# One gather in 64 of the first layer's ring becomes 128 single-row fetches issued by SyncE

## The reference, cut to what matters

```python
def _L0_gnn_ref(features, edge_src, edge_dst, edge_weight, W, b):
    msgs = features[edge_src] * edge_weight[:, None]
    agg = jax.ops.segment_sum(msgs, edge_dst, num_segments=N_NODES, indices_are_sorted=True)
    return jnp.einsum('ni,oi->no', agg, W) + b
...
x = x + _L0_gnn_ref(_layernorm(x, axis=-1), src, dst, edge_weight, L0_gnn_W, L0_gnn_b)
x = x + _L0_ffn_ref(_layernorm(x, axis=-1)[None], ...)[0]
```

## Time and profile before

| what | value |
|---|---|
| median of three runs | 6051.52 us (6050.52 to 6075.12) |
| the profiled execution | 6071.08 us, of which the span is 6069.4 us |
| gathers of layer 1 from `feats` | 1500, first at 165.7 us, last at 2957.7 us |
| rounds 2 to 23 | first hand-on at 286.4 us, last at 2916.1 us |
| layer 2's blocks with single rows | 3077 to 5768 us |

### The profile page before, as it was taken

One profiled execution on the slowest core, in us unless ns is written; L12 is line 12 of the kernel. 1 busy time (PEld: TensorE's weight loads), 2 busy tenths in 40 slices (PEclk: granted clock), 3 DMA queues, 4 the chain that ended last, 5 costly groups with the idle time before them and its releaser, 6 DMA issues. The chain is left out here.

```text
span 6069.4 us, 66499 instructions
## 1 busy us (share of the span) xinstructions
PE 3440.2 (57%) x13893; PEld 2630.0 (43%) x13894; DVE 2050.1 (34%) x6854; ACT 818.5 (13%) x2321; POOL 2688.8 (44%) x2801
## 2 busy tenths in 40 slices
PE   1444535455556667677832224982928376389927
PEld 0333323333434545455621013871807255277826
DVE  5445454545453444423300000330303012033436
ACT  3100000000000111111200000220202011022216
POOL 4554545454444555555377774026070613420050
PEclk5666666676777777888955556995959688699968
DMA  7422222222222333333201101121111111111137
GB/s 236 130 81 64 74 61 73 70 75 66 73 64 77 91 89 95 89 96 96 71 15 10 13 11 20 60 78 14 56 14 40 28 35 43 19 50 44 55 124 304
DMA packets 281484, 425.60 MB, mean 70 GB/s; under 512 B 64296, under 2 KB 215091, under 8 KB 280243
## 3 DMA queue, kind: packets, MB, share of 16 engines
q0 software_dynamic: 113696, 216.93, 13.9%
q1 hardware_dynamic: 69567, 114.91, 5.2%
q10 hardware_dynamic: 98004, 91.50, 4.7%
HBM read 317.12 MB, written 105.98 MB: 70 GB/s over the span
## 5 line engine op out<-in xcount | busy, mean ns | idle before, releaser
L692 POOL DMA_INDIRECT rows<-feats,src_t x1500 | 1432.4, 955 | 1393.7 <-PE node_sums L861 817.6
L1258 POOL DMA_INDIRECT got<-row_dram,src_sorted x1008 | 995.4, 988 | 1313.0 <-DMA state_dram<-got 1005.1
L861 PE MATMUL node_sums<-rows,ys_ahead 128*128 x3904 | 1171.9, 458 | 709.8 <-issue 548.7
L861 PEld LDWEIGHTS node_sums<-rows,ys_ahead 128*128 128x128 f32 x3904 | 859.0, 230 | 992.7 <-issue 856.0
L1352 PE MATMUL d_expert<-w,hid 128*128 128x256 f32 x3136 | 806.3, 398 | 557.8 <-issue 553.2
L1341 PE MATMUL d_hidden<-d_yt,w 128*128 128x256 f32 x3136 | 807.6, 399 | 525.6 <-issue 518.9
L1352 PEld LDWEIGHTS d_expert<-w,hid 128*128 128x128 f32 x3136 | 624.9, 199 | 710.6 <-issue 629.2
L1341 PEld LDWEIGHTS d_hidden<-d_yt,w 128*128 128x128 f32 x3136 | 622.8, 200 | 676.9 <-issue 600.4
L1404 DVE TENSOR_TENSOR yo<-d_expert,x_and_b 128x512 f32<-128x512 f32 x196 | 135.6, 692 | 2169.4 <-remote 1124.4
L1285 ACT ACTIVATE hid<-d_hidden,b1c 128x256 f32<-128x256 f32 x784 | 324.0, 471 | 2312.4 <-remote 1091.6
L920 DVE TENSOR_SCALAR ys_ahead<-iota,rel,ew_t 128x128 f32<-128x128 f32 x1952 | 566.7, 361 | 117.9 <-issue 50.1
(11 more groups left out here) (303 smaller groups left out, 2473.2 us busy)
## 6 DMA issues: line engine op xcount, KB each, us to landing
y_dram<-yo ACTq DMA_DIRECT2D x196, 256.0 KB
ys<-y_dram SPq DMA_DIRECT2D x36, 1024.0 KB
got<-row_dram SPq DMA_DIRECT2D x2048, 0.1 KB
rows<-feats,src_t POOLq DMA_INDIRECT x1500
got<-row_dram,src_sorted POOLq DMA_INDIRECT x1008
ys_ahead<-y_dram SPq DMA_DIRECT2D x13, 1024.0 KB
x_dram<-edge_plan ACTq DMA_DIRECT2D x98, 128.0 KB
d_x<-x_dram ACTq DMA_DIRECT2D x49, 256.0 KB
```

Of the source, the lines that this page charges most:

```text
L692: pool.indirect_dma_start(rows[:, g % RING, j, :], None, feats, bass.IndirectOffsetOnAxis(ap=m.src_t[:, g * GT + j:g * GT + j + 1], axis=0 ...
L861: t = pe.matmul(psA[:, ds(((code >> 1) & 1) * 512, FEAT)], hot[:, r, j, :], rows[:, ds((code >> 2) & (RING - 1), 1), j, :], start=False, s ...
L1258: pool.indirect_dma_start(got[:, k, j, 0:ROWF], None, m.row_dram, bass.IndirectOffsetOnAxis(ap=m.src_sorted[:, BEGIN[b] + j:BEGIN[b] + j + ...
```

## The change

Of every slot 15 in rounds 2 to 23 POOL leaves out the gather of column 3 (22 gathers fewer). SP fetches these 128 rows of 1 KB instead. At the head of a round it loads the 128 node numbers from `src` into `node_row_of`. After it has handed on slot 2 it waits until slot 15 is free (`s_free`) and the numbers have landed, and then reads ten numbers into registers and issues ten row DMAs behind the hand-on of each of the slots 2 to 13, and eight behind that of slot 14. Before it hands on slot 15 it waits for three gathers and for the 128 rows.

That slot 15 is free is told by POOL. Ahead of the refill of slot 3 of the same round it waits until PE has finished the group that last used slot 15 (group g - 4 counted from the group g that it is about to refill), and raises `s_free`.

```diff
+ROW_SLOT, ROW_COL, ROW_FROM, ROWS_A_GROUP = 15, 3, 2, 10
...
+            def ask_nodes(i):
+                sp.dma_start(node_row_of, src_cols[ds(i * (RING * GT) + (ROW_SLOT * GT + ROW_COL), 1), :]
+                             ).then_inc(s_wr, 16)
+
+            def single_rows(a, z):
+                _, nodes = nc.values_load_multi_w_load_instructions(
+                    node_row_of[0:1, a:z], engines=[mybir.EngineType.SP], min_val=0, max_val=NODES - 1,
+                    skip_runtime_bounds_check_because="edge_index names nodes")
+                for n, node in enumerate(nodes):
+                    sp.dma_start(rows[a + n:a + n + 1, ROW_SLOT, ROW_COL, :], feats[ds(node, 1), :]
+                                 ).then_inc(s_rows, 16)
...
             with sp.Fori(2, full_rounds) as i:
+                ask_nodes(i)
                 for k in range(RING):
-                    sp.wait_ge(s_got[k], i * (16 * GT) + 16 * GT)
+                    if k == ROW_SLOT:
+                        sp.wait_ge(s_got[k], i * (16 * (GT - 1)) + (16 * GT + 16))
+                        sp.sem_inc(s_past, 1)
+                        sp.wait_ge(s_rows, i * (16 * P) - 16 * P)
+                    else:
+                        sp.wait_ge(s_got[k], i * (16 * GT) + 16 * GT)
                     sp.sem_inc(s_ready, 1)
+                    if k == ROW_FROM:
+                        sp.wait_ge(s_free, i)
+                        sp.sem_inc(s_past, 1)
+                        sp.wait_ge(s_wr, i * 16)
+                        sp.sem_inc(s_past, 1)
+                    a = (k - ROW_FROM) * ROWS_A_GROUP
+                    if 0 <= a < P:
+                        single_rows(a, min(a + ROWS_A_GROUP, P))
...
+            def by_row(g):
+                return g % RING == ROW_SLOT and 2 <= g // RING < full_rounds
+
             def gather(g):
                 for j in range(GT):
+                    if j == ROW_COL and by_row(g):
+                        continue
...
+            def row_slot_free(g):
+                end = pool.value_load(m.group_end[0:1, g - RING:g - RING + 1], min_val=1, max_val=STEPS)
+                pool.wait_ge(s_mm, end)
+                pool.sem_inc(s_free, 1)
...
             for g in range(RING, GROUPS):
+                if by_row(g + RING - ROW_FROM - 2):
+                    row_slot_free(g + RING - ROW_FROM - 2)
                 refill(g)
```

More of the change, by code:

```diff
@@ L169, in build @@
             opening = layernorm_and_plan(nc, sem, x, src, dst, edge_weight, feats, m)
-            weighted_sums(nc, sem, opening, feats, edge_index, x, W, b, W_gat, att_src, att_dst, W1, b1, W2, b2, m)
+            weighted_sums(nc, sem, opening, feats, src, edge_index, x, W, b, W_gat, att_src, att_dst, W1, b1, W2, b2, m)
         attention_and_experts(nc, sem, m)
@@ L258, in layernorm_and_plan @@
         s_scale = sem("a_scale")
-        s_clear = sem("a_x_cleared")
+        s_clear = m.s_clear = sem("x_cleared_then_row_slot_free")
         s_var, s_std, s_norm = sem("a_var"), sem("a_std"), sem("a_norm")
@@ L503, in spread, with weighted_sums @@
                             m.node_dst[:, t, :], None).then_inc(m.s_sc, 16)
-def weighted_sums(nc, sem, opening, feats, edge_index, x, W, b, W_gat, att_src, att_dst, W1, b1, W2, b2, m):
+def weighted_sums(nc, sem, opening, feats, src, edge_index, x, W, b, W_gat, att_src, att_dst, W1, b1, W2, b2, m):
     XS = 4
@@ L571, in weighted_sums @@
         zeros = lent(512)
+        node_row_of = lent(P)[0:1, :].bitcast(I32)
         std = sb("std_all", [P, TILES])
@@ L585, in weighted_sums @@
         s_pc = sem("b_pool_const")
-        s_wr = sem("b_w_loaded")
+        s_wr = sem("b_w_and_row_nodes_loaded")
+        s_free, s_rows = m.s_clear, sem("b_rows_landed")
         s_w, s_wt, s_wte = sem("b_weights"), sem("b_w_turned"), sem("b_w_ready")
@@ L672, in _ @@
             sp.dma_start(m.state_dram[GEDGES:GEDGES + P, :], zeros[:, 0:STATE]).then_inc(s_zo, 16)
+            src_cols = src[0:(ETILES - 1) * P].rearrange("(c e) -> c e", e=P)
+            def ask_nodes(i):
[8 more added lines that the diff above has]
+                                 ).then_inc(s_rows, 16)
+            sp.wait_ge(s_wr, 16)
             with sp.Fori(2, full_rounds) as i:
+                ask_nodes(i)
                 for k in range(RING):
-                    sp.wait_ge(s_got[k], i * (16 * GT) + 16 * GT)
-                    sp.sem_inc(s_ready, 1)
+                    if k == ROW_SLOT:
[4 more added lines that the diff above has]
+                        sp.wait_ge(s_got[k], i * (16 * GT) + 16 * GT)
+                    sp.sem_inc(s_ready, 1)
+                    if k == ROW_FROM:
[6 more added lines that the diff above has]
+                        single_rows(a, min(a + ROWS_A_GROUP, P))
             for k in range(left):
```

## The result

The changed kernel takes 6998.33 us (median of four runs, 6987.31 to 7011.4), the kernel before 6058.89 us beside it. The ratio is 1.1553, with a 95% interval of 1.1529 to 1.1578: 939 us more. The profiled execution has a span of 7000.8 us.

The account below looks back on a forecast made before the run. Layer 1 was taken as bound by PE's chain and POOL's gathers obstructing each other. A round became 79 (run) + 63 (quiet time) + 5 (hand-over) = 147 us; 22 rounds add 604 us: 6656 us, range 6216 to 7041.

Parts of the forecast that it names:

- What bounds before: Layer 1: bound by PE's chain, about 91 us a round undisturbed, and POOL's gathers obstructing each other; a round takes 119.5 us.
- 22 gathers fewer: POOL, layer 1: 27.5 us of issue time removed, worth nothing to at most 41 us because POOL has slack.
- POOL's new wait makes one run of 79 us: Behind the wait ahead of slot 3, POOL issues 63 gathers in one run, 1.25 us each.
- In the run SP gets 27 rows out: During POOL's run: 12 rows in the first 16 us, then 15 at 4.2 us; PE has had five of 16 groups.
- The quiet time: While POOL stands still: PE's remaining 63 us cover SP's 101 rows (50 us); hand-over adds 4 us and POOL's start 1.
- the sum as written: A changed round in layer 1: 79 + 63 + 5 = 147 us; over 22 rounds 3234 us against 2630.
- Loading the node numbers at nothing: SP, once a round: the load is asked for while PE works on the last group 15, so it costs nothing.
- The rule weighed: The skill's rule that starting a DMA is usually small would hide SP's part; the trace disagrees beside gathers, 4.2 against 0.5 us.
- (1): Rival: SP's rows stay hidden under POOL's run and only 1.25 us a round goes; 6024 us, 8%.
- (2): Rival: the stage goes by the gather, 1.87 us each, 22 saved, -41 us; 6010 us, 4%.
- (3): Rival: slowness outlasts each run as in layer 2, 21.5 us instead of 4; 7041 us, 13%.

## Why the prediction was right or wrong

The direction held and 6998 lies in the range, near its upper end; the size did not: +604 us foretold, +939 measured. That the range held is in part luck: its upper end, 7041, was made with 21.5 us of slow time behind each run, and not that but SP's rows and the end of the round filled the room.

- **What bounds before**: PE and the gathers obstruct each other. Shown: with gaps between gathers PE's "issue" time goes from 519.8 to 7.5 us.
- **22 gathers fewer**, 0 to 41 us: 16 us measured. Right.
- **POOL's new wait makes one run of 79 us**: 17 of the 22 runs behind the wait stay whole (63 gathers with no pause of 6 us between them), and these take 78.7 to 82.0 us, 79.6 in the round above. Right.
- **In the run SP gets 27 rows out, 4.2 us apart, and PE five groups.** These 17 runs have 21 to 26 rows each, and in the round above most lie 3.5 to 4.9 us apart; PE's 43 matmuls are five steps and a little, about four groups at 22 steps for the 16 groups of such a round. Right, with a few rows and one group too many.
- **The quiet time: 63 us, PE's, with SP's 50 us under it, plus 5 us of hand-over.** This is the step that failed: the rows that the run leaves over were put at nothing beyond PE's chain, and the hand-over was too small. The quiet time is 84 us in the mean (164 less 80) and 78.9 in the round above. There the end of the slow time takes 7.6 us (to 2562.3), 101 rows with their loads 61 us (to 2623.3), landing and group 15 with its tile's stages 9 us (to 2632.2), POOL's start 1.4 us. I set PE's chain against SP's rows and took the longer. But PE gets each group only behind ten rows, so it walks at SP's pace ("SPq L701"), and group 15 can't begin before the last row has landed: the end of the slow time, the rows, group 15 and POOL's start follow each other. In size: SP's 50 us were 61, as long as PE's whole 63 us, since a row takes 0.41 us and each load of ten registers 1.1 or 2.3 us more (the 20 rows gave 0.5 with loads of eight); the hand-over of 5 us was 7.6 + 9 + 1.4 = 18 us, more than three times as much. In the early rounds the wait is longer still, up to 100.5 us (1711.0 to 1811.5); I have no run that tells DVE's sort from PE there.
- By the sum as written the rows were free and the wait alone would give the same 147 us a round. Without rows the round is 150 us (20 rounds from 476.5 to 3471.8 us), of which 80 are the run and 70 the quiet time, against 63 + 5 foretold. So the sum was nearly right for the wait alone and left out what the rows add: 14 us a round, 6 points.
- **Loading the node numbers at nothing**: asked for at 2626.94, 6.7 us before POOL goes on; no row waits for it. Right.
- **The rule weighed.** In the run with the rows alone SP's queue is full, 127 us of 139, with nothing else changed, and it costs 4.9%. The Trainium skill ("DMA: Bandwidth & Descriptors", section "Issuing engines are not separate DMA queues") calls the time to start a DMA usually small against the DMA; this case disagrees: in the round above the last row has landed 1.2 us after its issue began (2622.94 to 2624.17), while a row takes 0.41 us to issue in the quiet time and 4.2 beside gathers.
- **Rivals.** (1) and (2) fell: rows are not hidden, and dropping the gathers gains 0.27%. (3) was right in kind: the slow time does outlast the run, by 8 us instead of 4, not by 21.5.

## What to carry to other kernels

Where gathers by GpSimd run beside other work, look at the length of their unbroken runs, not at GpSimd's slack: a wait that bunches them costs the others their time even if it adds no work and GpSimd is idle half of the time. Small DMAs put on the queue that also hands data on cost little here until the queue was full (1.1% at 77 us of 122, 4.9% at 127 of 139), so add up the queue's time per round at the pace beside the gathers, and then follow what each hand-on stands behind. Two chains that exchange a signal at every step did not hide each other here: to the slower one's time add what the other still has to do behind its last signal, instead of taking the longer of the two.

## What the runs showed of the hardware

- Gathers 1.25 us apart hold the instructions of PE and SP, also a semaphore increment that moves no data: 0.72 us each (median) instead of 0.06. With 1.3 us between gathers instead of 0.3 PE's "issue" time goes from 519.8 to 7.5 us, that of DVE on the steps' two lines only from 227.1 to 77.4; SP had no rows in that run. What it is that holds them the runs don't tell, nor whether it is the gap between gathers or their number in a time that matters: the pause changes both.
- The hold sets in late and ends late: in the round above SP's first ten rows come 0.6 to 1.5 us apart (2476.5 to 2485.2), only then 3.5 to 6.3 us, and the slowness ends 8 us after the last gather. In the 17 whole runs SP's rows are 0.6 us or less apart again 6 to 10 us after it.
- Ten registers are loaded in 1.13 or 2.25 us, in turn from load to load. The Trainium skill ("Runtime: NRT & Kernel Launch", section "Instruction fetch mechanics") gives about 200 ns for a register; that is near the longer of the two here, 225 ns, and nearly twice the shorter, 113 ns.
- Not tried: a pause between 0.3 and 1.3 us in the kernel before. The long pause frees PE and makes POOL the bound at 156 us a round, against 119.5 before; whether a shorter one beats the kernel before is open.
